# Query-times-key-state products moved into the key-state group, softmax moved up, and two queues reordered, in a gated slot attention with a feed-forward block

## The reference, cut to what matters

```python
e = exp(clip(n @ Ws, -32, 32))        # slot weights, n = layernorm(x)
c = 1 / cumsum(e, tokens)             # inverse running sum
ok = (q k^T masked) @ e  +  q @ hk    # hk: key state of earlier 128-token chunks
p = softmax(ok * scale * c)           # over the 64 slots
w = p * c
o = (w e^T masked) @ v  +  w @ hv     # hv: value state of earlier chunks
o = o * rsqrt(mean(o**2) + eps) * g_norm * silu(n @ Wg)
x = x + o @ Wo
x = x + ((silu(gate) * up) @ down) * scale   # feed-forward, weights rounded to fp8
```

## Time and profile before

| | us |
|---|---|
| median of 3 runs | 1351.48 |
| lowest and highest | 1348.45 and 1352.53 |
| profiled execution, its own time | 1351.25 |
| its span, first to last instruction | 1349.5 |
| PE busy | 1323.1 (98%) |
| weight loads of PE (PEld) busy | 1096.6 (81%) |
| DVE busy | 1054.4 (78%) |
| ACT busy | 426.6 (32%) |
| POOL busy | 137.9 (10%) |
| DMA, SyncE's queue | 45.5% of 16 engines' span |

### The profile page before, as it was taken

One profiled execution on the slowest core, in us unless ns is written; L12 is line 12 of the kernel. 1 busy time (PEld: TensorE's weight loads), 2 busy tenths in 40 slices (PEclk: granted clock), 3 DMA queues, 4 the chain that ended last, 5 costly groups with the idle time before them and its releaser, 6 DMA issues.

```text
span 1349.5 us, 24276 instructions
## 1 busy us (share of the span) xinstructions
PE 1323.1 (98%) x9287; PEld 1096.6 (81%) x9287; DVE 1054.4 (78%) x1675; ACT 426.6 (32%) x1283; POOL 137.9 (10%) x106
## 2 busy tenths in 40 slices
PE   6999999999999999999999999999999999999998
PEld 5788888788888888888788788878888878888887
DVE  8888888888888888888888888888778875535354
ACT  4333323332333233233323332333333333222221
POOL 3001101110120012001100110111110010000000
PEclk9999999999999999999999999999999999999999
DMA  6147555655665575556655665565333430000000
GB/s 187 40 106 167 123 121 127 163 114 116 147 135 121 115 167 126 126 117 156 132 132 121 152 133 119 118 158 124 87 92 84 124 109 0 32 1 31 0 32 32
DMA packets 500559, 144.58 MB, mean 107 GB/s; under 512 B 359648, under 2 KB 491616, under 8 KB 500448
## 3 DMA queue, kind: packets, MB, share of 16 engines
q1 hardware_dynamic: 500448, 143.08, 45.5%
HBM read 85.80 MB, written 57.21 MB: 106 GB/s over the span
## 4 chain that ended last, share of the span: by engine, by line
PE 78%; DVE 9%; SPq 5%; DMA 4%; issue 2%; ACT 1%; POOL 0%; DVEq 0%
PE bank L486 15%; PE bank L488 14%; PE bank L487 14%; PE bank L118 13%; PE bank L1659 6%; PE bank L726 3%; SPq L369 3%; PE bank L709 2%; PE bank L566 2%; PE bank L546 2%; DMA fp_weights<-q 2%; SPq L334 2%; DMA e_tokens<-k_tok_then_wT 1%; PE bank L645 1%; PE bank L714 1%
## 5 line engine op out<-in xcount | busy, mean ns | idle before, releaser
L486 PE MATMUL bank<-wvg_hi,xT_hi 128*128 128x512 f32 x512 | 206.6, 404 | 0.7
L488 PE MATMUL bank<-wvg_hi,xT_lo 128*128 128x512 f32 x512 | 199.9, 390 | 0.0
L487 PE MATMUL bank<-wvg_lo,xT_hi 128*128 128x512 f32 x512 | 199.7, 390 | 0.0
L786 ACT ACTIVATE a_and_v<-bank 128x256 f32<-128x256 f32 x128 | 49.2, 384 | 326.8 <-PE bank L488 326.8
L486 PEld LDWEIGHTS bank<-wvg_hi,xT_hi 128*128 128x128 f32 x512 | 96.2, 188 | 25.5 <-issue 4.2
L488 PEld LDWEIGHTS bank<-wvg_hi,xT_lo 128*128 128x128 f32 x512 | 96.1, 188 | 20.5
L487 PEld LDWEIGHTS bank<-wvg_lo,xT_hi 128*128 128x128 f32 x512 | 96.3, 188 | 17.8
L1103 DVE RECIPROCAL cT<-cT 128x512 f32<-128x512 f32 x32 | 107.0, 3342 | 0.0
L1048 POOL TENSOR_TENSOR rstd<-ssq,neg_half 128x8 f32<-128x8 f32 x32 | 52.4, 1638 | 490.9 <-DVE ssq L1151 490.9
L486 PE MATMUL bank<-wo_hi,oT_hi 128*128 128x512 f32 x256 | 99.8, 390 | 0.0
L488 PE MATMUL bank<-wo_hi,oT_lo 128*128 128x512 f32 x256 | 99.6, 389 | 0.0
(11 more groups left out here) (168 smaller groups left out, 3036.9 us busy)
## 6 DMA issues: line engine op xcount, KB each, us to landing
o_transposed<-o SPq DMA_DIRECT2D x27, 512.0 KB, 3.4
oT_lo<-o_transposed SPq DMA_DIRECT2D x108, 128.0 KB, 3.0
fp_weights<-q SPq DMA_DIRECT2D x28, 318.0 KB, 3.2
e_tokens<-k_tok_then_wT SPq DMA_DIRECT2D x31, 256.0 KB, 2.3
e_tok<-e_tokens SPq DMA_DIRECT2D x124, 64.0 KB, 2.3
c_tokens<-cT SPq DMA_DIRECT2D x31, 256.0 KB, 2.4
cT<-c_tokens SPq DMA_DIRECT2D x124, 64.0 KB, 2.3
w_slots<-p SPq DMA_DIRECT2D x27, 256.0 KB, 2.4
```

The lines of the kernel that those rows point to most:

```text
L486: pe.matmul(dst, w_hi, m_hi, start=(k == 0), stop=False)
L487: pe.matmul(dst, w_hi, m_lo, start=False, stop=False)
L488: last = pe.matmul(dst, w_lo, m_hi, start=False, stop=(k == n - 1))
L786: return act.activation(dst, src, ACT.Copy)
```

## The change

On PE the query-times-key-state products go from behind the key job into the group, and the group's order becomes: key sums of chunk 0, inner products of chunks 0 and 1, key sums 1, inner products of chunks 2 and 3, key sums 2, value-state parts, query times key state. DVE takes the softmax up before the low half of the earlier output; ACT makes the exponential before it copies k. `load_e` now waits for the value-state parts, since they are the last of the group that read e. On SyncE `load_w` follows `store_w` at once, ahead of `load_e`; Wk (`load_skq(pair, 1)`) goes from ahead of the e store to behind `load_w`. `split_vg` goes behind the copy of k on ACT.

```diff
@@ SyncE
         def load_e(nu):
             sp.wait_ge(s_est, 16 * nu)
-            sp.wait_ge(s_hkd, (CH - 1) * nu)
+            sp.wait_ge(s_hvd, nu)
...
             load_q8(u)
-            if i == 2:
-                load_skq(pair, 1)
             store_e(u + 1)
             if u in W_FAR:
                 store_w(u)
+                load_w(u)
+            if i == 2:
+                load_skq(pair, 1)
             load_e(u + 1)
-            if u in W_FAR:
-                load_w(u)
@@ TensorE, in unit
-            inner_ok(par, range(CH))
+            inner_ok(par, (0, 1))
             key_sums(u, 1)
+            inner_ok(par, (2, 3))
+            key_sums(u, 2)
             for c in range(CH - 1):
...
             mm.then_inc(s_hvd, 1)
-            key_sums(u, 2)
+            inter_ok(u)
             if u > FAR + 1:
...
-            pe.wait_ge(s_hk, 3 * (u + 1))
-            for c in range(1, CH):
-                for a in range(2):
-                    hs = slice(DK * a, DK * (a + 1))
-                    for h in range(2):
-                        ts, ds = slice(64 * h, 64 * (h + 1)), slice(c * P + 64 * h, c * P + 64 * (h + 1))
-                        mm = pe.matmul(ok_of[a][c][ts, :], qT[hs, ds], hk[hs, c - 1, :],
-                                       start=False, stop=True, skip_group_check=True)
-            mm.then_inc(s_ok, 1)
@@ ScalarE: slot_exp(u) is the wait for s_sub and the exponential of p
-            if i == 3 and not tail:
-                act.wait_ge(s_job, job_count(VG3, u, i))
-                for k in range(KT):
-                    split_vg(pair_of_next(u), k)
+            if not first:
+                slot_exp(u)
             if not last:
                 evac(KTJ, nu, ni)
...
-            act.wait_ge(s_sub, u + 1)
-            act.activation(p[:, :], p[:, :], ACT.Exp).then_inc(s_exp, 1)
+            if i == 3 and not tail:
+                act.wait_ge(s_job, job_count(VG3, u, i))
+                for k in range(KT):
+                    split_vg(pair_of_next(u), k)
@@ VectorE
             value_states(u)
-            if u > FAR + 1:
-                out_lo(u - 1, A)
-            elif u > 1:
-                far_lo(u - 2)
...
                               ALU.subtract).then_inc(s_sub, 1)
+            if u > FAR + 1:
+                out_lo(u - 1, A)
+            elif u > 1:
+                far_lo(u - 2)
```

More of the change, by code:

```diff
@@ L241, in attention @@
     ffn.place(projected=s_job, out_w_read=s_wl, weights_split=s_vgh, vg_lo=(s_vgl, s_vgl2), q_read=s_ok,
-              k_read=s_kb, scores=s_a, e_read=s_hkd, weights_done=s_b, w_ready=s_wm, inter_done=s_oi,
+              k_read=s_kb, scores=s_a, e_read=s_hvd, weights_done=s_b, w_ready=s_wm, inter_done=s_oi,
               w_transposed=s_trw, gated=s_oev, gates=s_g, out_transposed=s_tro, out_done=s_y, added=s_ya,
@@ L567, in inner_ok, with inter_ok @@
                                   start=(c == 0), stop=(c == 0), skip_group_check=True)
+        def inter_ok(u):
+            pe.wait_ge(s_hk, 3 * (u + 1))
+            for c in range(1, CH):
+                for a in range(2):
+                    hs = slice(DK * a, DK * (a + 1))
+                    for h in range(2):
+                        ts, ds = slice(64 * h, 64 * (h + 1)), slice(c * P + 64 * h, c * P + 64 * (h + 1))
+                        mm = pe.matmul(ok_of[a][c][ts, :], qT[hs, ds], hk[hs, c - 1, :],
+                                       start=False, stop=True, skip_group_check=True)
+            mm.then_inc(s_ok, 1)
         def out_transposes(u, banks):
@@ L879, in key_state, with slot_exp @@
             copy(hk[:, c, :], state_banks(u)[0][:, 0:M]).then_inc(s_hk, 1)
+        def slot_exp(u):
+            act.wait_ge(s_sub, u + 1)
+            act.activation(p[:, :], p[:, :], ACT.Exp).then_inc(s_exp, 1)
         def wT_evac(u):
@@ L1609, in _ @@
         sp.wait_ge(w["k_read"], UNITS - 1)
-        sp.wait_ge(w["e_read"], (CH - 1) * UNITS)
+        sp.wait_ge(w["e_read"], UNITS)
         load_down(2)
```

## The result

| us | before | after |
|---|---|---|
| median | 1351.12 (20 runs) | 1354.05 (20 runs) |
| lowest, and highest of the runs compared | 1347.79, 1353.77 | 1350.80, 1357.49 |
| profiled execution, its span | 1351.25, 1349.5 | 1352.13, 1350.4 |

The ratio is 1.0023 with a 95% interval of 1.0015 to 1.0031: the change made the kernel slower by 0.23%. That is less than the 0.3% that the prediction took as the least that can be told, but the interval lies clear of no change, and 1354.05 lies above the prediction's range of 1338 to 1353. One run of the kernel before took 1523.68 us and is in neither the highest of the runs compared nor the ratio. The profiled execution of after is one of its quicker ones; it shows 0.9 of the 2.9 us.

What follows compares the result with a forecast made beforehand. PE's own stream of matmuls plus the few places where it stands still was taken as the bound; gains of 1.6 + 2.6 + 1.0 = 5.2 us off 1351.25 gave 1346.0 us, range 1338 to 1353.

Steps and rivals of the forecast that it cites:

- Part 1: Products with hk moved into PE's group: 0.21 saved less 0.16 for waiting key sums, 0.05 us a unit, 1.6 us.
- the 0.05 for loads that are not hidden: PE's small tiles after a change from the full array: first loads not hidden, four records 0.16 against 0.116.
- Part 2: Softmax up on DVE, value-weight splits back on ACT: third units shorter, 2.6 us gained.
- All 0.37 go: Units 3 to 27: the 0.37 us that third units run longer goes seven times, 2.6 us, at worst half.
- Both cost nothing: The output's low half moved back on DVE and the copy of k behind the exponential still come in time.
- Part 3: w first in SyncE's queue, Wk behind it: 7.7 us of waits removed, 6.7 new, 1.0 us gained.
- The rule: PE loses what the Wk split starts later than 5.75 us before the value products' turn.
- 0.6 + 3.4 + 2.7 = 6.7: New waits before the value products: unit 18 0.6, unit 26 3.4, units 6 and 22 1.35 each; 2, 10, 14 nothing.
- tile shapes change for free: Rival on PE's group, or key sums don't wait: the group gives 5 to 11 us, time 1337 to 1342; chance 0.17.
- Wk comes in time: Rival on the queue: 2.4 us for both transfers, no wait left, 11.9 us gained, 1339.3; chance 0.15.
- The wait only moves: Rival: line 709's wait moves to line 726 in full, 7.7 back, group gains nil: 1348.7 or no change; chance 0.18.
- The slower rival: ACT stands in front of Wk in all seven second units, 13.8 us lost there; 4.5 us slower, 1355.8; chance 0.10.

Runs made afterwards that it cites:

- group_only: Kernel before with only the PE part of the change (with the e loads' wait on s_hvd): 1343.05 us, ratio 0.9944.
- wk_split_late: Changed kernel with its transfers kept; ACT splits Wk behind the evacuations of VG0 and VG1 instead of ahead: 1340.53 us, ratio 0.9920.
- last_lo_early: Changed kernel with the low half of the earlier output ahead of the softmax in the last unit alone: 1351.89 us, ratio 1.0008.
- k_before_c: Changed kernel with the four k loads ahead of the store of c in SyncE's queue: 1344.49 us, ratio 0.9953.
- softmax_only: Kernel before with only the ACT and DVE parts of the change: 1375.93 us, ratio 1.0207.

## Why the prediction was wrong, point by point

**Part 1, the group: right, term by term.** The group of unit 17 of the changed kernel on PE:

```profile
591.18 0.34 PE L554 MATMUL bank<-e_tok,k_tok_then_wT 128*64 128x64 f32 x4
591.35 0.64 PE L565 MATMUL bank<-e_tok,a_and_v 128*64 128x64 f32 x16
591.84 0.34 PE L554 MATMUL bank<-e_tok,k_tok_then_wT 128*64 128x64 f32 x4
592.01 0.64 PE L565 MATMUL bank<-e_tok,a_and_v 128*64 128x64 f32 x16
592.50 0.34 PE L554 MATMUL bank<-e_tok,k_tok_then_wT 128*64 128x64 f32 x4
592.67 0.83 PE L658 MATMUL bank<-a_and_v,e_tok 128*64 128x128 f32 x12
593.42 0.58 PE L576 MATMUL bank<-hk,qT 64*64 64x64 f32 x24
```

From L565 to the next key sum 0.49 passes where eight steps of 0.058 are 0.47, and the key sum's own four records take 0.17 instead of 0.12: 0.07 a wait, 0.14 a unit, for the 0.16 taken. From L658 to L576 0.75 passes, where six steps of 0.11 are 0.66: the drain of 0.09. The moved products take 0.51 us up to the next job, as they did in the old place, so the 0.05 for loads that are not hidden is in both; that it is 0.05 is not shown by itself. Ordinary units went from 32.23 to between 32.14 and 32.18, for the 0.05 forecast. Here the trace agrees with the Trainium skill, "TensorEngine Tiling (Array Packing)", Key Properties, also between two small tile shapes.

**Part 2: the size right, its cause not, and a cost missed in the last unit.** "All 0.37 go" holds (units 3 to 27, 0.46 with part 1's share). But group_only shows that the group does it; the softmax order was not needed for it. That the sum came out was luck as far as the softmax and the splits are concerned: the credit belonged to part 1. "Both cost nothing" holds in units 2 to 30 and fails in the last: 1.2 us, since I took the 8.3 us of a unit with a query job for all units.

**Part 3: the mechanism right, its reach too short.** Forecast for unit 18 were Wk's issue at 638.8, its split at 642.25 and the value products at 648.0; measured are 639.75, 643.10 and 648.92, in a unit that starts 0.8 us later, and the value products are 0.8 us late in it where 0.6 was forecast. The rule holds in all seven units: the value products start 5.8 us behind the split in units 6, 18 and 26, and on time where the split comes earlier.

The step that failed is the sum "0.6 + 3.4 + 2.7 = 6.7", which ended at the value products. At these it was too high: they are 3.4 us late in all. Unit 26 has 1.4 instead of 3.4, mostly because Wk, put at 4.9 us from issue to split, took 3.4 there, and unit 22 has nothing. What the sum left out is larger, 9.0 us behind the value products, at the slot job and, most of it, at the next group. I priced who waits for the mask and stopped there; behind the mask on the same engine stand gate VG2, which the slot job waits for, and the turn of c, and behind that in SyncE's queue the loads of k. In unit 18 DVE needs 8.6 us from the mask to its last gate (648.19 to 656.75), with gaps of 0.1 us at most: it catches up nothing, so the lateness reaches the slot job and the turn of c whole. The mask begins 24.9 us into the unit where wk_split_late has 21.3, the turn of c 29.5 where it has 25.3. So unit 18 pays again at the slot job (0.4 us) and at the next group (0.9 by the list), and the next group pays too in units 2, 10 and 14, taken at nothing, where the value products are in time and the turn of c is not. Measured 12.4 where 6.7 stood: 5.7 us on the wrong side.

From the forecast of 5.2 us gained to the 0.9 lost in the profiled executions there are 6.1 us. The second units are 5.7 of them, less 0.4 because the old waits were 8.1 and not 7.7; the last unit is 1.2 and unit 0 0.4; part 1 gave back about 0.7, with some 2.3 us gained for the 1.6 forecast. The other 1.9 us, up to the median of 1354.05, no profile itemises: the change's runs vary over 1350.8 to 1357.5, and nearly the same program, last_lo_early, takes 33.79 us in unit 2 of its profile where this one takes 32.81.

**The rivals.** That tile shapes change for free falls. "Wk comes in time" falls, at 3.0 to 3.4 us from issue to split in all seven units. "The wait only moves" falls too: the value products are 3.4 us late and not 7.7, and the group did gain. The slower rival named the right cause and the right units, and its 13.8 us for the second units are near the 12.4 measured, but by luck, for the path is wrong: it needed 4.9 us for every Wk, and k_before_c shows that most of the loss ran over the k loads instead (4.2 us are left of the 12.4). Wk itself took 3.35 us in unit 18 (639.75 to 643.10), where the forecast had 3.47; the 2.6 us estimated from the Trainium skill's "DMA: Bandwidth & Descriptors", Anatomy of one DMA, is again too short for this queue.

## What to carry to other kernels

Moving a transfer back in a queue is priced at the engine that waits for it in order: list what stands behind the waiting instruction, then what stands behind those, across engines and through the DMA queue, until a step has slack of its own. If the transfer itself is not urgent, move the instruction that waits for it, not the transfer. And a place that has room in the steady part has to be looked up again in the first and last rounds, where the work that gave it room is missing.

## What the runs showed of the hardware

In softmax_only PE stood for 3.6 us in the last unit, and its steps afterwards were 0.43 us instead of 0.23:

```profile
1083.70 0.58 PE L673 MATMUL bank<-hk,qT 64*64 64x64 f32 x24
1087.89 0.77 PE L486 MATMUL bank<-wo_hi,oT_hi 128*128 128x512 f32 x1 [3.62 <-DVE oT_lo L1082]
1088.45 0.63 PE L487 MATMUL bank<-wo_lo,oT_hi 128*128 128x512 f32 x1
1088.88 0.63 PE L488 MATMUL bank<-wo_hi,oT_lo 128*128 128x512 f32 x1
```

The stretches from 1076 on (start:end, length, busy time of PE, PEld, DVE, ACT and POOL, granted clock, DMA share, GB/s):

```profile
1076.00:1084.00 8.00, 7.47 (x103) 6.01 (x103) 3.78 (x8) 3.25 (x9) 1.04 (x1) 1.00 0.94 333
1084.00:1092.00 8.00, 4.38 (x30) 3.42 (x23) 6.63 (x12) 0.63 (x1) 0.00 (x0) 0.69 0.02 7
1092.00:1100.00 8.00, 8.00 (x52) 6.51 (x52) 2.26 (x4) 1.80 (x3) 0.00 (x0) 0.89 0.00 0
```

The granted clock was 0.69 on average over 1084 to 1092 us and 0.89 over the next 8, that is, the lower of the two levels (1.2 GHz) for part of each and 2.4 GHz again after. Over the 13 steps from 1087.89 to 1093.58 alone it was 0.50, the lower level throughout; they took 5.7 us where 13 steps of 0.23 are 3.0. The shorter waits left it at 1.00: the 0.6 us in unit 18 of this run, and the 1.07 us in the last unit of the changed kernel. A wait on PE can be paid more than once: here 3.6 us of standing still cost some 2.7 us more behind it.
